# Softmax attention: operand parts stored once and read by pairs of products, and group 0 taken through all chunks first

## The reference, cut to what matters

```
x = x + attention(layernorm(x))
attention(t): q, k, v = t @ W_qkv          # 16 heads of 8
              q, k = layernorm(q) * q_scale, layernorm(k) * k_scale
              p = softmax(q k^T / sqrt(8), causal);  out = (p v) @ W_out
```

## Time and profile before

| | |
|---|---|
| median of three runs | 1299.62 us (1299.5 to 1301.71) |
| the profiled execution, its own time | 1301.57 us |
| its span | 1299.8 us |
| granted TensorE clock, mean over the span | 0.84 |
| block 1 | 0 to about 52 us |
| attention (block 2) | about 52 to 515 us |

### The profile page before, as it was taken

One profiled execution on the slowest core, in us unless ns is written; L12 is line 12 of the kernel. 1 busy time (PEld: TensorE's weight loads), 2 busy tenths in 40 slices (PEclk: granted clock), 3 DMA queues, 4 the chain that ended last, 5 costly groups with the idle time before them and its releaser, 6 DMA issues. The chain is left out here.

```text
span 1299.8 us, 17329 instructions
## 1 busy us (share of the span) xinstructions
PE 994.5 (77%) x5802; PEld 497.3 (38%) x5802; DVE 903.7 (70%) x1529; ACT 508.2 (39%) x1042; POOL 400.1 (31%) x479
## 2 busy tenths in 40 slices
PE   5477898999999998686667665399975775459994
PEld 3222222222222313444553213166652444336663
DVE  6957889898898700889977996633347997653335
ACT  5244566787778665321021001033334211113333
POOL 3211111011111112254434442156643444226662
PEclk9557789899999976789768985599997986669997
DMA  5890000000000001412101211011122120101114
GB/s 131 174 189 13 2 1 1 1 2 2 2 1 2 2 2 36 158 58 73 33 1 41 65 40 33 12 34 44 42 55 81 35 63 8 33 17 43 42 43 114
DMA packets 52797, 56.16 MB, mean 43 GB/s; under 512 B 7957, under 2 KB 40093, under 8 KB 52701
## 3 DMA queue, kind: packets, MB, share of 16 engines
q1 hardware_dynamic: 47480, 44.78, 13.5%
q0 software_dynamic: 4992, 10.23, 2.9%
q10 hardware_dynamic: 240, 0.05, 0.0%
HBM read 37.94 MB, written 16.91 MB: 42 GB/s over the span
## 5 line engine op out<-in xcount | busy, mean ns | idle before, releaser
L714 DVE TENSOR_REDUCE mpart<-ps 128x2 f32<-128x1024 f32 (+3 forms) x320 | 325.2, 1060 | 63.0 <-PE ps L765 38.3
L827 ACT ACTIVATE arena<-ps 128x512 f32<-128x512 f32 (+3 forms) x640 | 292.5, 541 | 155.1 <-PE ps L782 145.7
L782 PE MATMUL ps<-arena 51*128 51x512 bf16 (+3 forms) x640 | 187.5, 386 | 17.0 <-ACT arena L827 8.8
L1057 POOL TENSOR_TENSOR arena<-arena 128x512 f32<-128x512 f32 x96 | 122.2, 1273 | 165.1 <-DVE arena L1110 163.3
L796 PE MATMUL ps<-arena,w 128*32 128x512 f32 (+3 forms) x1280 | 168.9, 603 | 4.6 <-ACT arena L827 3.7
L765 PE MATMUL ps<-arena 51*128 51x512 bf16 (+3 forms) x640 | 152.0, 388 | 23.3 <-DVE mpart L714 15.3
L684 POOL TENSOR_SCALAR_AFFINE_SELECT arena<-arena 128x512 f32<-128x512 f32 x64 | 40.6, 635 | 325.8 <-ACT arena L827 254.3
L1559 DVE COPY arena<-ps 128x128 f32<-128x128 f32 x78 | 22.8, 292 | 161.7 <-PE ps L1702 161.7
L1649 ACT ACTIVATE arena<-ps 128x512 f32<-128x512 f32 x78 | 46.6, 597 | 218.9 <-PE ps L1712 218.9
L782 PEld LDWEIGHTS ps<-arena 51*128 51x128 bf16 x640 | 50.3, 96 | 186.7 <-ACT arena L827 146.4
L1096 DVE TENSOR_TENSOR arena<-arena 128x512 f32<-128x512 f32 x62 | 102.0, 1645 | 12.3 <-ACT arena L1163 4.6
(11 more groups left out here) (261 smaller groups left out, 1479.6 us busy)
## 6 DMA issues: line engine op xcount, KB each, us to landing
w<-in_w SPq DMA_DIRECT2D x2, 2048.0 KB, 10.8
arena<-results SPq DMA_DIRECT2D x16, 256.0 KB, 5.1
arena<-g_v SPq DMA_DIRECT2D x15, 256.0 KB, 3.6
arena<-r_v SPq DMA_DIRECT2D x15, 256.0 KB, 3.6
arena<-l_v SPq DMA_DIRECT2D x15, 256.0 KB, 3.6
arena<-q_stack SPq DMA_DIRECT2D x8, 384.0 KB, 7.0
arena<-k_stack SPq DMA_DIRECT2D x8, 384.0 KB, 8.9
tokens<-arena SPq DMA_DIRECT2D x8, 256.0 KB, 2.4
```

The lines of the kernel that those rows point to most:

```text
L714: nc.vector.tensor_reduce(out=mpart[:, 2 * pl:2 * pl + 2, t, kc], in_=ps[:, bank:bank + 2, 0:width], axis=AX.X, op=ALU.max).then_inc(ring_ ...
L782: nc.tensor.matmul(ps[:, n % ST, off:CH], rows(Ks, j % 2, 2 * g + j // 2, kt * P, (kt + 1) * P), rows(Qs, j % 2, 2 * g + j // 2, c * CH + ...
L827: nc.scalar.activation(probs[:, n % 2, j[0], off:CH], ps[:, (GH * n + j[0]) % ST, off:CH], ACT.Exp, scale=float(HD) ** -0.5).then_inc(exp_ ...
L1057: nc.gpsimd.tensor_tensor(z[:, n % ZB, :], state[:, n % SB, :], q[:, c % 2, :], ALU.mult).then_inc(z_ready, 1)
```

## The change

Each part is stored once: `store` becomes one DMA from `parts[c]` to a DRAM tensor `sources`. `stack` becomes twelve DMAs, one for each pair of neighbouring products, side and operand; each loads 16 rows of 8 KB, eight from the part of the first product and eight from that of the second. The stacked operands are laid out by chunk first, so a row of a chunk is contiguous, and `PRODUCTS` is reordered. `STEPS` takes group 0 through chunks 0 to 3, and then groups 1, 2 and 3 of chunk 3, of chunk 2, 1 and 0.

```
-PRODUCTS = [(0, 0), (1, 0), (2, 0), (0, 1), (1, 1), (0, 2)]
+PRODUCTS = [(0, 0), (2, 0), (1, 0), (1, 1), (0, 1), (0, 2)]
...
-        stacks = [nc.dram_tensor(name, [NC, 2, MROW, PAIRS * CH], BF16, kind="Internal").ap() for name in ("q_stack", "k_stack")]
+        sources = nc.dram_tensor("sources", [NC, 2, PARTS, P, CH], BF16, kind="Internal").ap()
...
-            Qs, Ks = (... .rearrange("p (n t) -> p n t", n=PAIRS) for i in (0, 1))
+            Qs, Ks = (... .rearrange("p (c n t) -> p c n t", c=NC, n=PAIRS) for i in (0, 1))
...
                 def store(sp, c):
-                    row = PAIRS * CH
-                    for s in (0, 1):
-                        r = 0
-                        for n in (3, 2, 1):
-                            for side in (0, 1):
-                                half = slice(side * P // 2, (side + 1) * P // 2)
-                                if s == 0:
-                                    src = parts[c][half, s, 0:n, :]
-                                else:
-                                    src = parts[c][half, s, 3 - n:4 - n, :].to_broadcast([P // 2, n, CH])
-                                sp.dma_start(bass.AP(tensor=stacks[s].tensor, offset=((c * 2 + side) * MROW + r * HD) * row,
-                                                     ap=[[CH, P // 2], [HD * row, n], [1, CH]]), src).then_inc(stored[c], 16)
-                            r += n
+                    sp.dma_start(sources[c].rearrange("s r p t -> p (s r) t"),
+                                 parts[c].rearrange("p s r t -> p (s r) t")).then_inc(stored[c], 16)
 
                 def stack(sp, c):
-                    sp.wait_ge(stored[c], 16 * 12)
-                    for side in (0, 1):
-                        for dst, src in ((Qs, stacks[0]), (Ks, stacks[1])):
-                            sp.dma_start(dst[64 * side:64 * side + MROW, :, c * CH:(c + 1) * CH],
-                                         src[c, side].rearrange("r (n t) -> r n t", n=PAIRS)).then_inc(stacked[c], 16)
+                    sp.wait_ge(stored[c], 16)
+                    for n in range(0, len(PRODUCTS), 2):
+                        for side in (0, 1):
+                            for s, stack_of in enumerate((Qs, Ks)):
+                                first, second = PRODUCTS[n][s], PRODUCTS[n + 1][s]
+                                row = 64 * side + n * HD
+                                at = ((c * 2 + s) * PARTS + first) * P * CH + side * P // 2 * CH
+                                sp.dma_start(stack_of[row:row + 2 * HD, c].rearrange("r n t -> r (n t)"),
+                                             bass.AP(tensor=sources.tensor, offset=at, ap=[[(second - first) * P * CH, 2], [PAIRS * CH, HD],
+                                                                                           [1, PAIRS * CH]])).then_inc(stacked[c], 16)
...
-                STEPS = [(g, c) for c in range(NC) for g in (0, 1)] + [(g, c) for c in reversed(range(NC)) for g in (2, 3)]
+                STEPS = [(0, c) for c in range(NC)] + [(g, c) for c in reversed(range(NC)) for g in (1, 2, 3)]
...
-                                pe.wait_ge(stacked[c], 64)
+                                pe.wait_ge(stacked[c], 16 * 12)
```

More of the change, by code:

```diff
@@ L298, in softmax_attention @@
             QK = PAIRS * T // 2
-            Qs, Ks = (arena[:, i * QK:(i + 1) * QK].bitcast(BF16).rearrange("p (n t) -> p n t", n=PAIRS) for i in (0, 1))
+            Qs, Ks = (arena[:, i * QK:(i + 1) * QK].bitcast(BF16).rearrange("p (c n t) -> p c n t", c=NC, n=PAIRS) for i in (0, 1))
             at = 2 * QK
@@ L652, in set_maxima @@
                         row = 64 * (j % 2) + MROW
-                        eng.dma_start(Qs[row:row + PARTS, 2 * g + j // 2, c * CH:(c + 1) * CH],
+                        eng.dma_start(Qs[row:row + PARTS, c, 2 * g + j // 2, :],
                                       mrow[j * P // GH:j * P // GH + PARTS * TPC, :]).then_inc(max_set[j], 16)
@@ L748, in rows @@
                         def rows(stack, side, pair, a, z):
-                            return stack[64 * side:64 * side + KROWS, pair, a:z]
+                            return stack[64 * side:64 * side + KROWS, a // CH, pair, a % CH:a % CH + z - a]
                         def add_mask(side, out):
```

## The result

The changed kernel takes 1338.68 us (median of 4, 1336.35 to 1340.12), against 1300.61 us for the kernel before, measured beside it: ratio 1.0291, interval 1.0272 to 1.031. It is 38 us slower; forecast were 1357 us and a range of 1335 to 1440. The profiled execution has a span of 1338.4 us, 38.6 more than before.

The account below looks back on a forecast made before the run. TensorE bound it, with VectorE mid-attention; DMA only briefly. Chunk 3 at 182.5, plus 84.8 and 302.8, ended values at 570.1, +57.8 us: span 1301.57 to 1359.4, less 1.95 for the median, predicted 1357, range 1335 to 1440.

Parts of the forecast that it names:

- chunk 0, 1, 2 there: Times in us when each chunk's loads have landed for the attention; chunk 0's set the start of TensorE's maxima.
- a chunk's cycle: From one chunk's landing to the next: store 2.2, loads on two engines 33.3, landing 2.1, together 37.6 us.
- from there to the end of (0,3)'s values: Group 0, chunk 3: maxima 37.2, split, turn, DMAs and first exponential 7.7, values 39.9; 84.8 us in sum.
- The rate of an engine: In the stacked loads: each of two engines moves 23.6 GB/s, so a chunk takes 33.3 us.
- Chunk 3 ends last in each comparison: Chunk 3 lands at 182.5 us, after the maxima of (0,2) end at 178.9, and starts the remaining chain.
- The pace of the last steps: Three steps each of chunks 3, 2, 1 and 0 at the earlier trace's pace: 302.8 us, attention's values ending at 570.1.
- What I costed at nothing: Around the loads: block 1 ending after 60 instead of 52, and ScalarE's issues for steps 0 to 3, at no cost.
- the moved steps: Small-chunk steps moved to the attention's end: no cheaper there, costing 60.2 us.
- Rival A: Loads spread over all engines, so the new order leaves the cold start: 1291 to 1297 us; chance 0.13 with C.
- Rival C: Only the order matters, loads otherwise hidden, a wait on chunk 1 at 59: 1297 to 1300 us; counted in A's 0.13.
- Rival B: Loads on two engines at 9.3 GB/s each, 84.5 us a chunk: 1562 us; chance 0.07 with rates under 15.
- With four engines the waits are nearly gone: If a chunk's loads ran on four engines (16.7 + 4.3 us), TensorE's waits for chunks would almost vanish.

Follow-up runs that it names:

- order_alone: The kernel before with the new order of `STEPS` alone, stores and loads as they were: 1293.64 us, ratio 0.9959.
- after_turn_first: The changed kernel, with no maximum of steps 1, 2 and 3 planned before the turn of the previous step's maxima: 1336.29 us, ratio 1.0305.
- wide_source: The changed kernel with each load's source pattern counting 16 contiguous rows outermost, not 2 times 8 (other stacked contents): 1294.15 us, ratio 0.9965.

## Why the prediction was right, and by how much its terms were off

The direction, the mechanism and the place were right: two engines, a wait at each of the first three chunks, a share of 0.13 to 0.14. The measured 1338.68 us lies near the lower end of the range, which stood for 27 GB/s an engine and the warmer end; both came. The forecast of +57.8 us for the attention's end was 19.8 too much. By its own steps:

| step | predicted | measured |
|---|---|---|
| chunk 0, 1, 2 there | 69.7, 107.3, 144.9 | 65.6, 100.1, 135.1 |
| a chunk's cycle | 37.6 | 34.5 |
| maxima of (0,3) begin | 182.5, chunk 3 | 172.7, end of (0,2)'s maxima |
| from there to the end of (0,3)'s values | 84.8 | 85.8 |
| three steps of chunk 3 | 119.3 | 119.1 |
| of chunk 2 | 92.7 | 86.9 |
| of chunk 1 | 64.8 | 56.7 |
| of chunk 0 | 26.0 | 29.1 |
| end of the attention | 570.1 | 550.3 |

- *The rate of an engine* was mis-sized: 23.6 GB/s, the best mean over sixteen engines, against 26.5 (8 KB in 309 ns). By the packet records the packets of a chunk take some 30.8 us instead of 33.3, and what stands around them 3.7 instead of 4.3; this is the 3.1 us of each cycle.
- *"Chunk 3 ends last in each comparison"* failed. With the faster cycle it was there by about 170, where the DMA share drops to nothing, and the maxima of (0,2) ended after it, at 172.7. They took 37.6 us from chunk 2's arrival, not 34.0. The wait at chunk 3 that I had counted on was not there; together with the rate this is 9.8 us. The way from there to the end of (0,3) took 1.0 us more than predicted.
- *The pace of the last steps* is the other 11.0 (9.8 - 1.0 + 11.0 = 19.8). I took means of before, and one of before's two steps of chunk 1 had run with the clock at 0.50: 25.0 us of the 43.2. In the changed kernel the granted clock stays at 1.00 until 520, as maxima go on until 500 and the steps left over after them are small ones. I had named this as 3 us; it was 8 in chunk 1 and 6 in chunk 2, with 3 given back in chunk 0. The same back end in order_alone is its whole gain, so the better pace belongs to the order. That the clock is its cause fits the rows of chunk 1, and was not tested by itself; of chunk 2 it explains little, as before's slower step there (32.7 us against 29.1) had the clock at 0.84 for 11 us and at 1.00 for the rest.
- *What I costed at nothing*: block 1 did not end later (its last operation ends at 51.9; before, at 51.6). The turns stuck behind the loads were worth at most 3 us (after_turn_first).
- *A slip*: for the moved steps the prediction gives 60.2 us; its own terms (30.9, 21.6, 8.7) make 61.2. The sum does not use it.
- *Rival A* had the right size and side for an order whose loads spread: 1291 to 1297 predicted, 1294.15 in wide_source and 1293.64 in order_alone. That was luck in part: its front was some 7 to 12 us too short ((0,3) ends at 213, not at 201 to 206) and its back 12 us too long. *Rival C* gave the order alone 1297 to 1300, which was too slow. *Rival B*'s rate did not occur.
- "With four engines the waits are nearly gone": the loss was (1301.38, no difference from before), the wait for chunk 1 was not (14.0 us), and four engines cost about 7 us on sixteen.

## What to carry to other kernels

Before a transfer is reshaped to save bytes or transfers, read the outermost count of both its patterns: a source that is "two parts of eight rows" ran on two of sixteen engines, and with halved store traffic the kernel gained nothing, not even with the loads on sixteen engines. A DMA share near a small multiple of 1/16 while everything waits is the sign of it. The share itself is not a rate: sixteen engines at 0.98 moved 113 GB/s in loads of 16 rows, where the earlier trace rows has 378 at 1.10. An order that asks for the next chunk one step earlier needs a step that can fill the wait: with the loads of before, leaving one small step in place there made a gain of 0.4% one of 1%. The 38 us were the loads', and that step was not tried with them.

## What the runs showed of the hardware that was not expected

- The outer count set the engines at work: shares of 0.13, 0.25, 0.50 and 0.98 with 2, 4, 8 and 16.
- More engines helped only up to a point: 32.5, 17.9, 16.4 and 15.3 us for 1536 KB with 2, 4, 8 and 16 engines and loads of 16 rows; with eight engines and loads of 8 rows 25.4 us, with four and loads of 4 rows 21.0. Source rows that lie apart in DRAM change nothing (24.8 us). Past that point the engines stay busy and each packet takes longer: 0.31, 0.61 and 1.08 us for 8 KB with 4, 8 and 16.
- Each of two engines moved 26.5 GB/s, and each of four 26.8, more than the 23.6 that each of sixteen had in the earlier trace rows. Three engines that wrote three adjacent partitions moved 29 GB/s together, with packets of 32 KB or of 8.
